# Graph attention on one core: the mask bytes of the last 20 units turned by VectorE, from quarter loads

## What is computed

```
h   = max(layernorm(x), 0)
Wh  = h @ W
e   = leaky_relu((Wh @ a1)[:, None] + (Wh @ a2)[None, :], 0.2)
att = softmax(where(adj > 0, e, -9e15), axis=1)
out = x + elu(att @ Wh)
```

## Time and profile before

| | |
|---|---|
| median of 3 runs | 244.6 us (244.16 to 244.75) |
| the profiled execution | 244.79 us, of which the span of the trace is 243.0 |
| busy, share of the span | PE 93%, PEld 91%, DVE 81%, ACT 64%, POOL 24% |
| `words` L610 | 128, mean 1278 ns |
| `to_bytes` L420 | 63 of 128 x 2048, mean 1993 ns |
| `turn` L817 | 512 transposes, PE busy 34.3 us |
| products L834 to L836 | 3 x 1000 matmuls recorded, 171.9 us each group |
| transfers | 71.92 MB, mean 296 GB/s over the span |
| loads of `raw` | 64 of 1024 KB, 14.1 us from issue to landing (median) |

### The profile page before, as it was taken

How to read it: one execution, slowest core, us unless ns; L and a number is a source line. 1 busy time by engine, 2 the same in 40 slices (tenths; PEclk the granted TensorE clock), 3 DMA queues, 4 the chain that set the end, 5 groups by cost and what they waited for, 6 DMA issues and landing times.

```text
span 243.0 us, 8254 instructions
## 1 busy us (share of the span) xinstructions
PE 227.0 (93%) x3736; PEld 221.2 (91%) x3736; DVE 196.4 (81%) x259; ACT 156.2 (64%) x139; POOL 59.1 (24%) x48
## 2 busy tenths in 40 slices
PE   6969999599999999999999999999999999999970
PEld 2759899599998999999999999999999999999970
DVE  4999997536776998889887988898879888998864
ACT  3698836697799999944996677019975774000051
POOL 3648036897000070300000560000001710040000
PEclk9997999999999999999999999999999999999995
DMA  6999999999998999999999999999999300020002
GB/s 225 360 389 386 386 386 385 388 367 370 301 352 284 363 395 386 388 385 385 398 386 385 388 385 385 385 387 369 386 386 386 140 0 3 3 89 3 3 0 92
DMA packets 36521, 71.92 MB, mean 296 GB/s; under 512 B 1282, under 2 KB 1924, under 8 KB 36484
## 3 DMA queue, kind: packets, MB, share of 16 engines
q1 hardware_dynamic: 35520, 69.74, 79.0%
q10 hardware_dynamic: 964, 1.64, 1.8%
HBM read 69.27 MB, written 2.10 MB: 294 GB/s over the span
## 4 chain that ended last, share of the span: by engine, by line
PE 74%; ACT 8%; DVE 7%; issue 4%; POOL 4%; DMA 1%; ACTq 0%; DVEq 0%; POOLq 0%
PE acc L834 20%; PE acc L835 20%; PE acc L836 20%; PE mask_t L817 11%; ACT mask L420 4%; POOL v L330 2%; POOL val L333 2%; ACT neg L432 1%; DVE words L610 1%; DVE stats L547 1%; DMA x_sb<-in_x_dram 1%; PE acc L796 1%; PE acc L805 1%; ACT neg L511 1%; DVE wh_sb L573 1%
## 5 line engine op out<-in xcount | busy, mean ns | idle before, releaser
L610 DVE SCALAR_TENSOR_TENSOR words<-g_row,gq_word,mask_t 128x1024 f32<-128x1024 f32 x128 | 161.4, 1278 | 36.0 <-PE acc L836 19.0
L834 PE MATMUL acc<-val,words 128*128 128x129 f16 x1000 | 171.9, 220 | 0.3 <-DVE wh_sb L573 0.3
L835 PE MATMUL acc<-val,words 128*128 128x129 f16 x1000 | 171.9, 220 | 0.0
L836 PE MATMUL acc<-val,words 128*128 128x129 f16 x1000 | 171.9, 220 | 0.0
L420 ACT ACTIVATE mask<-raw,step_bias 128x2048 uint8<-128x2048 int32 x63 | 121.8, 1993 | 28.4 <-DVE x_sb L626 17.3
L834 PEld LDWEIGHTS acc<-val,words 128*128 128x128 f16 x1000 | 97.8, 98 | 0.5 <-issue 0.5
L835 PEld LDWEIGHTS acc<-val,words 128*128 128x128 f16 x1000 | 97.9, 98 | 0.1
L836 PEld LDWEIGHTS acc<-val,words 128*128 128x128 f16 x1000 | 97.8, 98 | 0.0
L817 PE MATMUL mask_t<-ident_b,mask 128*128 128x128 bf16 x512 | 34.3, 221 | 1.8 <-ACT mask L420 1.8
L817 PEld LDWEIGHTS mask_t<-ident_b,mask 128*128 128x128 bf16 x512 | 30.3, 99 | 2.2 <-ACT mask L420 2.2
L358 POOL TENSOR_TENSOR hp<-num,rz 128x1024 f32<-128x1024 f32 x3 | 5.7, 1897 | 105.3 <-DVE rz L621 105.3
(11 more groups left out here) (91 smaller groups left out, 125.4 us busy)
## 6 DMA issues: line engine op xcount, KB each, us to landing
raw<-in_adj_dram SPq DMA_DIRECT2D x64, 1024.0 KB, 14.1
x_sb<-in_x_dram SPq DMA_DIRECT2D x8, 256.0 KB, 5.7
out_dram<-x_sb ACTq DMA_DIRECT2D x3, 512.0 KB, 7.9
out_dram<-x_sb SPq DMA_DIRECT2D x2, 128.0 KB, 2.4
out_dram<-x_sb SPq DMA_DIRECT2D x1, 192.0 KB, 1.9
w_sb<-in_L_gnn_W_dram ACTq DMA_DIRECT2D x1, 64.0 KB
out_dram<-x_sb SPq DMA_DIRECT2D x1, 64.0 KB, 1.6
a_sb<-in_L_gnn_a_dram ACTq DMA_DIRECT2D x1, 1.0 KB
```

The source lines that it names most:

```text
L610: nc.vector.scalar_tensor_tensor(words[:, q], g_row[:, c * CHUNK:(c + 1) * CHUNK], gq_word[:, 1, t:t + 1], maskt_bytes[:, u % 2, q // 2, : ...
L834: nc.tensor.matmul(acc_tile(t), high, val[:, tile, 0, 0:V], start=first and t % PT == 0, stop=False, skip_group_check=True)
L835: nc.tensor.matmul(acc_tile(t), high, val[:, tile, 1, 0:V], start=False, stop=False, skip_group_check=True)
L836: last = nc.tensor.matmul(acc_tile(t), low, val[:, tile, 0, 0:V], start=False, stop=False, skip_group_check=True)
```

## The change

Units 0 to 11 (`NA` = 12) are loaded, turned and multiplied as before. Units 12 to 31 come in five sets of four: a set is 1024 rows x 2048 columns. Member `h` of a set is now loaded as 256 rows x 2048 columns: partition group `k` of 32 gets columns `512 k` to `512 k + 511`, 8 rows on each partition. That is four DMAs of 0.5 MB, each to 32 partitions, two issued by SP and two by ACT (`load_set`), ACT's behind its conversion of the unit three before in the load order. ACT makes bytes of the four members into one of two buffers of a whole set (the old `mask` buffer, and `second`, which lies over `h_t` and `v32`). DVE then turns unit `n` with one `transpose` of 128 x 1024 four-byte words in squares of 32, reading every fourth word (a step of 16 bytes) from that buffer and writing `mask_t` (`turn_set`); its first in a set waits for the bytes of all four members. It stands before the last words of the unit before. The words read single bytes 4 apart (before: 2 apart).

The loads' order is 0 to 7, then 8, 12, 9, 13, 10, 14, 11, 15, then 16 to 31; ACT makes bytes in the same order.

Since in a set the order of the rows of `adj` and of `val` differs from before, `val` is moved once (eight DMAs of 128 x 2560 bytes within SBUF, `move_values`) to `val_set`, which lies over `x_sb`. So a chunk's rows of `x` are read again from HBM before its result (`load_rows`), the rows of chunks 1 to 3 have another order in memory (their `g_row` is copied with steps), and each chunk's result goes where those rows lie. The last chunk is stored with three DMAs instead of four.

The core of the diff:

```diff
@@ set-up
+    NA = U + U // 2
+    LOADS = [*range(U)] + [n for i in range(4) for n in (U + i, NA + i)] + [*range(NA + 4, C * U)]
+    AT = [LOADS.index(n) for n in range(C * U)]
+    adj_set = adj.rearrange("(c h r t) (s k j) -> c s h k r t j", h=4, r=QUARTER, t=CT, k=4, j=BLOCK)
...
@@ sync
+            def load_set(n):
+                i = AT[n] % RING
+                for k in SP_QUARTERS:
+                    sp.dma_start(raw[k * QUARTER:(k + 1) * QUARTER, i], adj_set[n // U, n % U // 4, n % 4, k]).then_inc(set_in[i], 16)
...
-            for n in range(1, C * U):
...
+            for at in range(1, C * U):
+                n = LOADS[at]
+                if n >= NA:
+                    sp.wait_ge(act_bytes, 2 * (at - RING) + 1)
+                    load_set(n)
+                else:
...
+                if at == U + 1:
+                    sp.wait_ge(vl_first, 2)
+                    sp.wait_ge(vl_ready, G - 1)
+                    sp.wait_ge(pad_ready, 2)
+                    sp.wait_ge(ht_ps, NB)
+                    for b in range(4, NB):
+                        move_values(b)
+                if at == U + 3:
+                    for b in range(4):
+                        move_values(b)
+                if at == U + 4:
+                    sp.wait_ge(words_free, 6 * BT)
+                    sp.wait_ge(val_moved[1], 4 * 16)
+                    load_rows(0)
+                if at == 2 * U:
+                    sp.wait_ge(words_free, U * BT)
+                    load_rows(1)
+                if at == 22:
+                    sp.wait_ge(out_early[0], 16)
+                    load_rows(2)
+            sp.wait_ge(out_early[1], 16)
+            load_rows(C - 1)
...
@@ gpsimd
+            nc.gpsimd.memset(val_word[:, :, :, V // 2:VP // 2], 0.0).then_inc(pad_clear, 1)
...
@@ scalar
+            def set_to_bytes(n):
+                i, h, slot_in = (n - NA) // 4, n % 4, AT[n] % RING
+                act.wait_ge(set_in[slot_in], 64 * FILLED[n])
+                if i == 0:
+                    act.wait_ge(vl_ready, G - 1)
+                    act.wait_ge(wh_ps, 3 * G)
+                elif i == 1:
+                    act.wait_ge(turned, U + h + 1)
+                else:
+                    act.wait_ge(set_turned, 4 * (i - 1))
+                for k in range(2):
+                    nc.scalar.activation(set_bytes[i % 2][:, h, k * BT:(k + 1) * BT], raw[:, slot_in, k * BT:(k + 1) * BT], ACT.Sign,
+                                         scale=1.0, bias=step_bias[:, 0:1]).then_inc(act_bytes, 1)
+            def load_set(at):
+                if at >= C * U or LOADS[at] < NA:
+                    return
+                n, i = LOADS[at], at % RING
+                act.wait_ge(act_bytes, 2 * (at - RING) + 1)
+                for k in ACT_QUARTERS:
+                    act.dma_start(raw[k * QUARTER:(k + 1) * QUARTER, i], adj_set[n // U, n % U // 4, n % 4, k]).then_inc(set_in[i], 16)
...
+            for at in range(U, C * U):
+                n = LOADS[at]
+                if n < NA:
+                    for k in range(2):
+                        to_bytes(1, n % U, k)
+                else:
+                    set_to_bytes(n)
+                load_set(at - 1 + RING)
+                if at == 14:
+                    tail(0)
+                if at == 16:
+                    store(0)
+                if at == 23:
+                    tail(1)
+                if at == 27:
+                    store(1)
...
@@ vector
+            def turn_set(n):
+                i, m = (n - NA) // 4, n % 4
+                if m == 0:
+                    dve.wait_ge(act_bytes, 2 * AT[n + 3] + 1)
+                dve.wait_ge(words_ready, 4 * (n - 1))
+                nc.vector.transpose(maskt_quads[:, n % 2].rearrange("p (t h r) -> p t h r", h=4, r=QUARTER),
+                                    set_quads[i % 2].rearrange("p (h t j m) -> p m t h j", h=4, t=CT, m=4)[:, m]).then_inc(set_turned, 1)
...
                     for q in range(BT):
+                        n = c * U + u
+                        if q == BT - 1 and NA <= n + 1 < C * U:
+                            turn_set(n + 1)
                         weights(c, u, q)
                         if (u, q) == (0, 2):
                             take_sums(c - 1)
-                        if (u, q) == (4, 3):
+                        if (u, q) == ((3, 2) if c == 1 else (4, 3)):
                             result(c - 1)
...
@@ tensor
-                        turn(c, u + 1)
+                        if c * U + u + 1 < NA:
+                            turn(c, u + 1)
```

More of the change, by code:

```diff
@@ L48, in bass_graph_attention @@
     U = NB
+    NA = U + U // 2
+    LOADS = [*range(U)] + [n for i in range(4) for n in (U + i, NA + i)] + [*range(NA + 4, C * U)]
+    AT = [LOADS.index(n) for n in range(C * U)]
+    FILLED = [len([m for m in LOADS[:AT[n] + 1] if AT[m] % RING == AT[n] % RING and (m < NA) == (n < NA)]) for n in range(C * U)]
     V = F + 1
@@ L159, in bass_graph_attention @@
         raw_in = [[sem(f"raw_in{s}_{k}") for k in range(2)] for s in range(RING)]
+        set_in = [sem(f"set_in{h}") for h in range(RING)]
+        set_turned = sem("set_turned")
+        pad_clear = sem("pad_clear")
+        pad_ready = sem("pad_ready")
+        val_moved = [sem(f"val_moved{k}") for k in range(2)]
+        rows_in = [sem(f"rows_in{c}") for c in range(C)]
         first_bytes = sem("first_bytes")
@@ L210, in bass_graph_attention @@
         out_done = sem("out_done")
+        out_early = [sem(f"out_early{c}") for c in range(2)]
         squares_ready = sem("squares_ready")
@@ L824, in product @@
                 tile = u * BT + q
+                if n in (NA, 2 * U) and q == 0:
+                    pe.wait_ge(val_moved[u // 4], 4 * 16)
+                v = val if n < NA else val_set
                 for t in range(CT):
@@ L833, in product @@
                     low = words_h[:, q, t * P:(t + 1) * P, LO]
-                    nc.tensor.matmul(acc_tile(t), high, val[:, tile, 0, 0:V], start=first and t % PT == 0, stop=False, skip_group_check=True)
-                    nc.tensor.matmul(acc_tile(t), high, val[:, tile, 1, 0:V], start=False, stop=False, skip_group_check=True)
-                    last = nc.tensor.matmul(acc_tile(t), low, val[:, tile, 0, 0:V], start=False, stop=False, skip_group_check=True)
+                    nc.tensor.matmul(acc_tile(t), high, v[:, tile, 0, 0:V], start=first and t % PT == 0, stop=False, skip_group_check=True)
+                    nc.tensor.matmul(acc_tile(t), high, v[:, tile, 1, 0:V], start=False, stop=False, skip_group_check=True)
+                    last = nc.tensor.matmul(acc_tile(t), low, v[:, tile, 0, 0:V], start=False, stop=False, skip_group_check=True)
                     if (u, q) == (U - 1, BT - 1) and t in (2, 5):
```

133 lines of the change are left out of this document (90 added, 43 removed).

## The result

The median rose from 244.68 us (244.16 to 244.79, 4 runs) to **305.2 us** (303.81 to 305.91, 4 runs): ratio 1.247, 95% interval 1.242 to 1.253. The profiled execution took 303.81 us, its span is 302.0. The forecast was 250.9 with a range to 271.5: the sign was right, the size was not.

What follows compares the result with a forecast made beforehand. TensorE bound the kernel before, DVE after. Unit 12's first word at 115.4 plus 122.7 of DVE gives 238.1; + 11.8 - 0.6 = 249.3 us span, + 1.8 - 0.2 = 250.9 us; range 240.5 to 271.5.

Steps and rivals of the forecast that it cites:

- Part 1: TensorE no longer turns units 12 to 31: 17.8 us saved if TensorE stayed the bound.
- Part 2: DVE's transpose takes 1.16 us (1.13 to 2.13), making DVE the bound at 5.93 us a unit; saving shrinks to 2.9 us.
- S: Start of unit 12's first word on DVE: forecast 115.4 us, range 111.6 to 117.0, against 105.58 before.
- X: End of DVE's last words: forecast 238.1 us, against 231.20 before.
- rival A: DVE's stepped transposes take two cycles an element, 2.13 us: 19.4 us more, 270.3 us; chance 0.17.
- Part 3: When unit 12 can start, given interleaved loads and ACT's bytes: 9.8 us lost.
- 14.9 MB at 386 GB/s: Transfers after 60 us until unit 11's load closes, moves of values and a read of x included: 38.5 us.
- Part 4: Small edits: DMA issues, waits and copies cost nothing, final stores save some 0.6 us, TensorE keeps its clock.
- The supply that I had named for later sets: Loads stay ahead of DVE at 5.43 us a unit; quarter loads under 350 GB/s would become the bound.
- B: 32-partition loads are slow; first form: half rate whenever the other queue has none, 14 us, 265 us, chance 0.12.
- Its second form: The two queues' 32-partition loads never add up, 20 units at 10.9 us: 343 us, chance 0.05.
- C: Faster: DVE's words save 5.0 us with bytes 4 apart, and loads arrive earlier: together 240.4 us; chance 0.22.

Runs made afterwards that it cites:

- experiment 6: Plain load order 0 to 31: in the changed kernel 289.24 us; with 128-partition loads, neighbouring-word transposes and values copied by POOL 246.01 us against 249.39.
- experiment 4: Kernel with 128-partition loads and neighbouring-word transposes, its moves of values going to 128 partitions instead of 32: 256.33 us against 268.71.
- experiment 1: Changed kernel with the set loads going to 128 partitions instead of 32: 281.43 us.
- experiment 3: Changed kernel with values copied by POOL instead of moved by DMA: 283.04 us; also with 128-partition loads and neighbouring-word transposes: 249.39 us.
- experiments 5 and 9: Changed kernel with SP loading quarters 0 and 2, ACT 1 and 3: 331.33 us; SP loading all four: 347.17 us. The other is the repaired kernel.
- experiment 7: ACT issues its half of a load before its two conversions: 305.35 us in the changed kernel, 287.56 us with plain load order.
- (8): Changed kernel with the read of chunk 0's rows of x placed behind load 15 instead of load 12: 305.03 us.
- the repaired kernel: Changed kernel with plain load order, transposes reading 128-byte runs, values sorted by POOL: 270.15 us; with SP's wait and row read behind load 15: 256.6 us.

## Why the prediction was wrong

**Part 1** held: no turning on TensorE after unit 11, and DVE became the bound, as forecast. It did not pay in any kernel that I ran: the best that the idea reached is the 246.01 us of experiment 6.

**Part 2, the mis-sized term is the transpose.** I took 1.16 us from start to start, the rate of one-cycle operations, and called the stepped rows too few; it was 1.97. The 19 transposes between S and X make 19 x 0.81 = 15.4 us of the 15.1 by which that stretch came out longer (the words cost 1.18 to 1.19, as the earlier trace rows said), all twenty 16.2. The upper end, 2.13 us, was nearly right, and so was rival A in itself (19.4 us more). The Trainium skill ("Advanced Engine Details and Errata", Memory Cachelines) was right for this instruction: 2.10 us at a 16-byte step, 1.25 in runs of 128 bytes. Stepped rows of eight elements had pointed the right way, and I chose by size of instruction where I should have chosen by how it reads.

**Part 3, the step that failed is "14.9 MB at 386 GB/s".** That rate belongs to transfers that have 128 partitions wherever they touch SBUF. Of the 38.2 us that S came late, the 32-partition ends of loads and moves carry 32.2 (153.72 - 121.51, experiment 4). The other 6.1 are loads that were late for other reasons (3.6, of them 1.7 lost before 60 us) and the steps behind unit 11's bytes (2.5, mostly the clock). Taken out one at a time, the quarter loads are worth 22.4 (experiment 1) and the moves 20.9 (experiment 3); they overlap by some 4, since both gone give 39.0 (153.72 - 114.72). Of the moves the prediction had counted only the bytes: 2.62 MB, 6.8 us at 386 GB/s, and they cost about that with 128-partition ends (6.8, experiment 4).

**Part 4** held in its issues and stores: ACT's issues hide behind activations, and behind X lie 10.6 us against 11.2. The supply that I had named for later sets, 350 GB/s, was there for most of them (369 from 160 us, 321 from 180, 371 from 210 to 240), and DVE never waited for bytes from S on. One step failed: TensorE did not keep its clock. 0.68 was granted from 100 to 120 us, where it was busy 4 us of 20, and 0.50 when it turned unit 11, in front of S. That cost 1.5 us there (experiment 4), which the prediction had put at nothing. Behind S DVE is the bound and the clock (0.91 from 180 to 200 us) costs nothing.

**Rivals.** A held. B held in its first form, as far as experiments 5 and 9 show it (one half of the partitions receives while the other queue has nothing for the other half), with 22.4 us instead of 14. Its second form, queues that never add up, would have needed the quarters split differently: 371 GB/s against 219. C fell: words with bytes 4 apart take 1.18 to 1.19 us, against 1.19 before. My larger error of method was to give A and B chances as if only one could come true. Both did, and a third cost that I had no rival for, the moves, came on top.

**What stays open.** Why quarter loads reach 371 GB/s late but 226 to 275 between 80 and 160 us in the changed kernel. That ACT's half comes late is excluded (experiment 7), and so is the place of the row read (8). The moves alone don't do it: without them the rate is 261 to 284 GB/s from 80 to 140 us (experiment 3). Whole loads and quarter loads alternate on SP's queue there, and without the alternation S is 17.5 us earlier (experiment 6); that the alternation itself unbalances the two halves is what I would suspect, and it wasn't isolated. In the repaired kernel the cause of the slow stretch is shown: with the one wait moved, 219 and 210 GB/s became 311 and 319.

## What to carry to other kernels

- A GB/s figure belongs to the partitions at both ends of the transfer. Before you cut a tile into 32-partition pieces, price them at the rate of one half (some 220 GB/s here), and count on more only while two queues write different halves all the time.
- Choose the row for an unseen operation by its access pattern, not by its size, and if runs can be made (128 bytes), reorder the data rather than step through it.
- Check a sum on a kernel that has every term at the price forecast, not on one that lacks a term: two errors can cancel.
- Uncertain costs that don't exclude each other must be added in the range. And a wait put into the list of an engine that issues loads holds back every load behind it: 18 us of SP standing still cost 13.5 us of the kernel.

## What the runs showed of the hardware that I had not expected

- Two queues with 32-partition loads reach 371 GB/s when one keeps to partitions 0 to 63 and the other to 64 to 127, 236 when their quarters share halves, and one queue alone 219; the same bytes over 128 partitions run at 386 to 391.
- A move of 320 KB within SBUF from 128 partitions to 32 landed after 13.7 us among wide loads, one to 128 partitions after 8.3 us.
- A 32-square transpose of 128 x 1024 four-byte words to PSUM: 2.10 us with a 16-byte step between the words read, 1.25 us with contiguous words or runs of 32.
- TensorE was granted 0.50 of its clock (1.2 GHz) after it had waited 15.87 us; the first words behind it came 3.99 us after the start of its turning instead of 2.53.
